# A gated attention and feed-forward stage: two interleaved streams become two half-programs, with taps and biases on TensorE

## The reference

```python
x1 = x + oT.T @ WoT0 + bo0                      # output of the cross attention before
n  = layernorm(x1)
q, k = elu(n @ Wq + bq) + 1, elu(n @ Wk + bk) + 1     # 16 heads of 16, per batch of 64 rows
v, g = n @ Wv + bv, sigmoid(n @ Wg + bg)
x1 = x1 + (g * (q @ masked_by_head(k.T @ v))) @ Wo + bo
xq = act_quant(layernorm(x1))                   # rounded to 127 / max|row|
h  = xq @ weight_quant(w1).T                    # 1024 wide
h  = silu(conv_w[:,0]*h[t-1] + conv_w[:,1]*h[t] + conv_w[:,2]*h[t+1] + conv_b)   # depthwise over 64 rows
x2 = x1 + act_quant(h) @ weight_quant(w2).T
q3 = layernorm(x2) @ Wq3 / 4                    # queries of the next stage
```

## Time and profile before

| | before |
|---|---|
| median of three runs | 3895.37 us (3893.12 to 3897.8) |
| profiled execution | 3894.62 us |
| its span, first to last instruction | 3892.6 us |
| granted TensorE clock over the span | 0.892 |
| busy: TensorE, VectorE, ScalarE, GpSimd | 3063.7, 2590.2, 1971.4, 620.4 us |

### The profile page before, as it was taken

One profiled execution on the slowest core, in us unless ns is written; L12 is line 12 of the kernel. 1 busy time (PEld: TensorE's weight loads), 2 busy tenths in 40 slices (PEclk: granted clock), 3 DMA queues, 4 the chain that ended last, 5 costly groups with the idle time before them and its releaser, 6 DMA issues. The chain is left out here.

```text
span 3892.6 us, 99208 instructions
## 1 busy us (share of the span) xinstructions
PE 3063.7 (79%) x34478; PEld 2671.8 (69%) x34478; DVE 2590.2 (67%) x7538; ACT 1971.4 (51%) x4188; POOL 620.4 (16%) x741
## 2 busy tenths in 40 slices
PE   3449999999999964555379999999999999643574
PEld 3348888888888853443268888888888888532453
DVE  5558888888888836666666777776777777465001
ACT  1146766666666632223246666666666666421111
POOL 0223333333333210000121111111111111000101
PEclk7669999999999986777679999999999999865787
DMA  2123223233333220000111111111111111212511
GB/s 66 50 82 84 82 79 85 80 82 83 81 82 83 67 62 11 22 22 11 36 32 42 38 42 39 38 40 40 39 38 41 38 42 28 73 44 69 191 48 61
DMA packets 235433, 221.17 MB, mean 57 GB/s; under 512 B 69516, under 2 KB 228545, under 8 KB 234816
## 3 DMA queue, kind: packets, MB, share of 16 engines
q1 hardware_dynamic: 232896, 208.22, 18.9%
q0 software_dynamic: 2048, 6.68, 0.5%
HBM read 186.30 MB, written 28.39 MB: 55 GB/s over the span
## 5 line engine op out<-in xcount | busy, mean ns | idle before, releaser
L1892 DVE CUSTOM_DVE_ANT_0 xb_junk<-xb_ring,xb_mbias 128x372 bf16<-128x372 f32 (+2 forms) x1024 | 543.6, 573 | 177.6 <-PE xb_ring L1800 158.0
L1731 ACT ACTIVATE xb_P<-xb_sc 124x1024 f32<-124x1024 f32 (+1 forms) x416 | 426.0, 1026 | 374.5 <-PE xb_sc L1824 372.6
L879 PE MATMUL xa_acc<-xa_raw,xa_P 124*128 124x193 f32 x1664 | 315.6, 331 | 7.7 <-ACT xa_P L754 7.7
L1771 PE MATMUL xb_ring<-xb_xst,xb_whi 128*128 128x372 f32 (+2 forms) x768 | 262.4, 369 | 38.6 <-DVE xb_xst L1871 32.8
L1800 PE MATMUL xb_ring<-xb_khi,xb_qhi 64*128 64x372 f32 (+2 forms) x1024 | 269.8, 404 | 26.4 <-DVE xb_klo L1877 17.3
L1771 PE MATMUL xb_ring<-xb_whi,xb_xst 128*124 128x256 f32 (+1 forms) x1248 | 285.3, 291 | 2.9 <-DVE xb_maxes L1892 0.6
L1824 PE MATMUL xb_sc<-xb_qhi,xb_khi 64*124 64x256 f32 (+1 forms) x1664 | 282.4, 372 | 0.0
L879 PEld LDWEIGHTS xa_acc<-xa_raw,xa_P 124*128 124x128 f32 x1664 | 266.4, 189 | 19.1 <-ACT xa_P L754 12.1
L1877 DVE TENSOR_TENSOR xb_klo<-xb_ring,xb_khi 128x372 fp32r<-128x372 f32 (+2 forms) x256 | 138.8, 572 | 208.7 <-ACT xb_khi L1697 207.7
L865 PE MATMUL xa_sc<-xa_qblk,xa_kT 128*124 128x128 f32 x1664 | 238.6, 272 | 0.0
L1771 PEld LDWEIGHTS xb_ring<-xb_whi,xb_xst 128*124 128x124 f32 (+1 forms) x1248 | 215.8, 187 | 23.0 <-DVE xb_maxes L1892 15.6
(11 more groups left out here) (418 smaller groups left out, 8222.9 us busy)
## 6 DMA issues: line engine op xcount, KB each, us to landing
xa_raw<-in_ctx SPq DMA_DIRECT2D x64, 279.0 KB
ex_w<-in_W SPq DMA_DIRECT2D x16, 1024.0 KB, 8.8
xa_raw<-in_ctx SPq DMA_DIRECT2D x32, 372.0 KB
xa_xTr<-in_ctxT SPq DMA_DIRECT2D x64, 186.0 KB
xb_raw<-in_ctxT SPq DMA_DIRECT2D x64, 186.0 KB
xa_xTr<-in_ctxT SPq DMA_DIRECT2D x32, 248.0 KB
xb_raw<-in_ctxT SPq DMA_DIRECT2D x32, 248.0 KB
xa_mask<-in_mask SPq DMA_DIRECT2D x32, 200.1 KB, 5.2
```

The costliest lines, as they stand in the source:

```text
L879: i = nc.tensor.matmul(acc[:, o, :], w, raw[0:KEYS, t3, t, :], start=t == 0 and o == 0, stop=t == NKT - 1, skip_group_check=True)
L1731: nc.scalar.activation(P[0:w, pbuf(c, p), :], sc[(c + p) % 2][0:w, :], ACT.Exp).then_inc(sem("exped"), 1)
L1771: i = nc.tensor.matmul(out, l, r, start=k == 0, stop=k == 4)
L1892: v.tensor_tensor_reduce(out=junk[:, k, 0:w], in0=ring[f % 3][:, 0:w], in1=mbias[:, p, k0:k0 + w], scale=1.0, scalar=-3.0e38, op0=ALU.add, ...
```

## The change

The streams and rounds go. All eight groups are written out, each as two half-programs, `attention(g)` and `ffn(g)`, and on every engine the halves of neighbouring groups are merged: each half is a generator that yields a planned time before every piece, attention of group g begins at 32g and its ffn at 32g + 31.5, and `by_time` always lets the half with the earliest next time go on. Attention has the banks pA to pD, the ffn pE to pH.

Work moves between engines. The biases of keys, values, gate and both output projections become a third matmul per tile (`row0`, one row of ones, against the bias). The three taps of the convolution become float32 matmuls with diagonal matrices `taps`, which GpSimd builds once. Elu reads PSUM on ScalarE (exp and relu), sigmoid and Silu become tanh: ScalarE writes y and tanh(y/2) from PSUM, VectorE multiplies y (1 + tanh); the factor 2 is taken out in the scales. GpSimd computes the power -0.5 of the variance in ln's and exp's place, and the rounding of the second quantization. The maximum over the ffn's values is taken in two halves. Loads come in two parts, `first` for attention and `later` for the ffn.

```diff
@@ helpers
+def by_time(*works):
+
+    nexts = [(begin + next(work), k) for k, (begin, work) in enumerate(works)]
+    while nexts:
+        _, k = at = min(nexts)
+        nexts.remove(at)
+        begin, work = works[k]
+        t = next(work, None)
+        if t is not None:
+            nexts.append((begin + t, k))
...
@@ gated_attention_and_ffn
+    EVERY, SECOND = 32, 31.5
...
+        def biased(out, xT, name, b):
+            for t in range(GROUP):
+                for k in range(2):
+                    nc.tensor.matmul(out[:, t, :], xT[:, k, TOK * t:TOK * t + TOK], wm[name][:, k, :], start=k == 0, stop=False)
+                i = nc.tensor.matmul(out[:, t, :], row0[:], bias[b][:], start=False, stop=True)
+            return i
+
+        def groups(*parts):
+
+            works = []
+            for g in range(NG):
+                works += [(g * EVERY + begin, part(g)) for begin, part in zip((0, SECOND), parts)]
+            by_time(*works)
...
@@ GpSimd
+                nc.gpsimd.tensor_tensor(b.rstd[:], b.var[:], mhalf[:], ALU.pow).then_inc(sem(tag + "_rstd"), 1)
...
+                    for f in range(NF):
+                        for k in range(3):
+                            i = nc.gpsimd.tensor_scalar(taps[:, f, k], ident[:], conv[:, f, k:k + 1], None, ALU.mult)
...
+                    nc.gpsimd.tensor_scalar(h2q[:, f:f + 2], h2r[:, f:f + 2], ROUND, ROUND, ALU.add, ALU.subtract).then_inc(sem("h2q"), 1)
...
@@ ScalarE
+                act.wait_ge(sem("k_ps"), g + 1)
+                nc.scalar.activation(ke[:], tok(pD), ACT.Exp)
+                nc.scalar.activation(kb[:], tok(pD), ACT.Relu).then_inc(sem("ke"), 1)
...
+                nc.scalar.activation(gb[:], tok(pB), ACT.Tanh, scale=0.5).then_inc(sem("gb"), 1)
...
-                    nc.scalar.activation(b.h2[:, f, :], b.cv[:, f % 3].rearrange("p b s -> p (b s)"), ACT.Silu).then_inc(b.sem("h2"), 1)
...
+                for f in range(NF):
+                    yield 5.2 + 1.7 * f
+                    act.wait_ge(sem("c_ps"), g * NF + f + 1)
...
+                    nc.scalar.activation(h2[:, f, :], c_bank(f), ACT.Identity, bias=conv[:, f, 3:4])
+                    nc.scalar.activation(th[:, f % 2], c_bank(f), ACT.Tanh, scale=0.5, bias=halfb[:, f:f + 1]).then_inc(sem("th"), 1)
...
@@ TensorE
+                for f in range(NF + 1):
+                    if f < NF:
+                        yield 3 + 1.7 * f
...
+                        for k in range(2):
+                            i = nc.tensor.matmul(h_bank(f), w1q[:, k, 128 * f:128 * f + 128], xqT[:, k, :], start=k == 0, stop=k == 1)
+                        i.then_inc(sem("h_ps"), 1)
+                    if f:
+                        yield 2.7 + 1.7 * f
+                        pe.wait_ge(sem("hs"), g * NF + f)
...
+                        for k in range(3):
+                            i = nc.tensor.matmul(c_bank(f - 1).rearrange("p (b s) -> p b s", s=S), taps[:, f - 1, k],
+                                                 padded[:, (f - 1) % 3, :, k:k + S], start=k == 0, stop=k == 2)
+                        i.then_inc(sem("c_ps"), 1)
...
@@ VectorE
-                v.tensor_tensor(b.kb[:], tok(b.pD), wide("bk"), ALU.add).then_inc(b.sem("kb"), 1)
...
-                v.tensor_tensor(b.vb[:], tok(b.pA), wide("bv"), ALU.add).then_inc(b.sem("vb"), 1)
...
-                    b.chain.step(v.scalar_tensor_tensor(out=b.cv[:, f % 3], in0=b.padded[:, f % 3, :, 0:S], scalar=conv[:, f, 0:1], in1=b.cv[:, f % 3], op0=ALU.mult, op1=ALU.add))
-                    v.scalar_tensor_tensor(out=b.cv[:, f % 3], in0=b.padded[:, f % 3, :, 2:S + 2], scalar=conv[:, f, 2:3], in1=b.cv[:, f % 3], op0=ALU.mult, op1=ALU.add).then_inc(b.sem("conv"), 1)
...
+                for f in range(NF):
+                    yield 3.7 + 1.7 * f
...
+                    v.tensor_tensor(padded[:, f % 3, :, 1:S + 1], h_bank(f).rearrange("p (b s) -> p b s", s=S),
+                                    srow[:].rearrange("p (b s) -> p b s", s=S), ALU.mult).then_inc(sem("hs"), 1)
+                    yield 6.2 + 1.7 * f
+                    dve.wait_ge(sem("th"), g * NF + f + 1)
+                    v.scalar_tensor_tensor(out=h2[:, f], in0=th[:, f % 2], scalar=1.0, in1=h2[:, f], op0=ALU.add, op1=ALU.mult).then_inc(sem("h2"), 1)
+                    if f == 5:
+                        yield 6.4 + 1.7 * f
+                        dve.wait_ge(sem("h2"), g * NF + NF // 2)
+                        v.tensor_reduce(top[:, 0], h2[:, 0:NF // 2].rearrange("p f t -> p t f"), AX.X, ALU.max, apply_absolute_value=True)
...
```

More of the change, by code:

```diff
@@ L1121, in _, with load @@
[L1121 to L1129 removed]
+            def load(g):
+                sp.dma_start(xs[:, g % 2], tiles_of(x, g)).then_inc(sem(f"x_in{g % 2}"), 16)
+                sp.dma_start(os_[:, g % 2], halves_of(oT, g)).then_inc(sem(f"x_in{g % 2}"), 16)
@@ L1131, in _ @@
+            load(0)
+            for dst, src in first:
+                sp.dma_start(dst, src).then_inc(sem("first_in"), 16)
+            for dst, src in later:
+                sp.dma_start(dst, src).then_inc(sem("later_in"), 16)
+            groups(attention, ffn)
+            for p in range(2):
+                sp.wait_ge(sem(f"x2_out{p}"), 16 * (NG // 2))
+                sp.wait_ge(sem(f"q3_out{p}"), 16 * (NG // 2))
         @block.gpsimd
         def _(pool):
+            nc.gpsimd.memset(row0[:], 0.0).then_inc(sem("zero"), 1)
@@ L1291, in work @@
[L1291 to L1297 removed]
+                i.then_inc(sem("y2_ps"), 1)
+                yield 34
+                pe.wait_ge(sem("c_norm"), g + 1)
+                transpose_group(nc, dim(pG), ln2, ident).then_inc(sem("l2_ps"), 1)
@@ L1298, in _ @@
+                yield 36
+                pe.wait_ge(sem("lT2"), g + 1)
+                by_dim(nc, dim(pG), lT2, wm["Wq3"]).then_inc(sem("q3_ps"), 1)
+            groups(attention, ffn)
         @block.vector
@@ new lines, in _, with variance @@
+            dve.wait_ge(sem("first_in"), FIRST)
+            dve.wait_ge(sem("set"), 1)
+            def variance(b, tag, X):
+                for t in range(GROUP):
+                    i = v.bn_stats(b.stats[:, t, :], X[:, t, :])
+                chain.step(i)
+                wait_apart(dve)
+                for t in range(GROUP):
+                    i = v.bn_aggr(b.moments[:, t, :], b.stats[:, t, :])
+                chain.step(i)
+                v.tensor_scalar(b.var[:], b.moments[:, :, 1], LN_EPS, None, ALU.add).then_inc(sem(tag + "_var"), 1)
@@ new lines, in ffn @@
+                for t in range(GROUP):
+                    i = v.scalar_tensor_tensor(out=X[:, t, :], in0=tok(pG)[:, t, :], scalar=s2[:, t:t + 1], in1=X[:, t, :], op0=ALU.mult, op1=ALU.add)
+                i.then_inc(sem("x2"), 1)
+                dve.wait_ge(sem("x2"), g + 1)
+                variance(nb2, "c", X)
+                yield 32
+                if g:
+                    dve.wait_ge(sem("l2_ps"), g)
+                normed(nb2, "c", X, ln2, g + 1)
+            groups(attention, ffn)
```

647 lines of the change are left out of this document (342 added, 305 removed).

## The result

The changed kernel takes **3959.3 us** in the median (3955.49 to 3961.17), against 3895.39 of the kernel before on the same chip: ratio 1.0162, 95% interval 1.0149 to 1.0174. It is slower, as forecast, but by 64 us where 24 were forecast, and outside the range.

A forecast was written before the change was run, and what follows sets the result against it. No engine was full; in the new order VectorE's program order would run eight tiles serially. The stage, 58 - 1.7 + 7 x 58.4 + 60.8 = 525.9 us against 502.0, gives +24: 3919 us, range 3880 to 3950.

The forecast's parts named there:

- Serial tiles: In the ffn's convolution, eight tiles run one after the other through three engines, 3.35 us each.
- From the first tap to Wo's residual add: Per group: 28.1 us for the eight tiles, 9.5 from there through Wo, and 1.2 for the clock.
- The 1.2 for Wo's clock: TensorE may lose its clock level ahead of Wo: +1.2 us per group, a mean of 0 and 2.6.
- From the diagonal to the first tap: Per group: diagonal 0.5 us, broadcast and y-projection 3.4, transposes to hidden pairs 3.9, y at half clock 2.5.
- GpSimd gets the rounding: Rounding 512 columns on GpSimd costs 0.61 us, four per group beside VectorE's row scalings; some 0.1 shows per group.
- the third rival: GpSimd decides: a power of 1.6 us exposed twice and the port, period 62, +49 us, 3944; chance 0.15.
- Wrong would make it: Signs against the forecast: tiles under 2.5 us apart, a power over 1.6 us, or a clock of 1.0 throughout.
- 24 of 0.3: At the stage's start, GpSimd builds 24 tap diagonals of 0.3 us ahead of the first power, ending at 27.5.
- The power: GpSimd's power -0.5 on 128x2: taken as 0.4 us, between 0.2 and 1.6, behind two roundings.
- The contention: VectorE's two-SBUF-input products wait for GpSimd's SBUF reads: 1.2 us per group by the rule, 0.3 by the measured row.
- The tail: The last group's ffn, with nothing beside it, up to the next stage: 60.8 us, 6.8 of it to its first taps.
- Costed at nothing: ... the bias matmuls, except ...: Bias matmuls cost nothing except between tiles 3 and 6 and in y and Wo, 0.86 us each.

The follow-up runs named there:

- e3: The changed kernel with VectorE's scaling of tile f+1 put ahead of the gating product of tile f: 3918.1 us, ratio 1.0056 to the kernel before.
- e4: The changed kernel with twelve added matmuls per group whose result nobody reads, between Wo and the next diagonal: 3939.6 us, ratio 1.0109 to the kernel before.
- e8: The changed kernel without the rounding of h2, the row scaling writing the BF16 tile directly (another result): 3923.4 us, ratio 1.0064 to the kernel before.
- e6: The changed kernel without the ten bias matmuls of a group (result lacks five projections' biases): 3929.9 us, ratio 1.0081 to the kernel before.

## Why the prediction was right in kind and wrong in size

The mechanism was right and one term of the sum far too small: what the work on GpSimd costs.

- **Serial tiles** (3.35 us): right, 3.28; e3 shows that the order causes it. The eight tiles with attention beside them were forecast at 28.1 and took 27.9.
- **From the first tap to Wo's residual add**, 28.1 + 9.5 + 1.2 = 38.8: measured 1853.23 - 1814.52 = 38.7. The 1.2 for Wo's clock was a mean of 0 and 2.6; Wo took 1.0 more than at full clock, 3.6 for 2.6, since its first half runs at half clock and its second at full. No line of the forecast names that case, so this agreement is luck in part.
- **From the diagonal to the first tap**, 0.5 + 3.4 + 3.9 + 2.5 = 10.3: measured 9.9. The clock's term was right: y at half clock, and e4 gives 2.1 of the 2.5 back.
- **"GpSimd gets the rounding": this step failed.** "A cast of 744 columns is 807 ns ... 512 columns are 0.61, and four lie beside VectorE's row scalings", with 0.1 exposed. Measured: 1.92 to 2.23 us, and 3.6 exposed per period (12.86 against 9.3), 8.1 in the tail. The rows of the cast are of one operation; this instruction has two (add, then subtract). The rounding was given one price and no upper end, though the text bounds the power from both sides: the upper end of 63 for a period has 3 us for all of GpSimd, and the third rival gives them to the power and the port. Nor is it among the signs of "Wrong would make it", none of which came. With e8's 33.0 us added, and the 0.7 that is there already taken off, the sum would have been about 3951.
- **"24 of 0.3": the same step at the start.** 0.58 each. The first power starts 1468.10 - 1432.97 = 35.1 us behind the first load, for 27.5: the late loads are in at 21.0 for 19.5, and the taps take 14.1 for 8.0 (24 of 0.3 are 7.2, so the 27.5 is 0.8 high by its own terms). So 6.1 of the head's 7.6 are the taps and 1.5 the loads; from the power to the diagonal it is 30.5, as forecast. The line through casts of 744 and 992 columns was carried down to 128. With these 7.6 on top of the 3951 it would have been 3959, and 3959.3 was measured; that it is so near is luck in part, since terms that were too high and too low cancel in the rest.
- **The power**: priced 0.4, measured 0.69 to 0.82, within its bounds; it is late mainly because it queues behind a rounding.
- **The contention** was worked out at 0.3 us per group and then left out of the sum, where 58.4 has 0.1 for all of GpSimd. The three row scalings grew from 1.89 (e8, which writes BF16; one alone takes 0.69 in both) to 2.30, the one-input pair L1438 from 0.73 to 1.43, and the small product L61 from 0.15 to 0.56. The Trainium skill (SBUF — State Buffer, Who interferes with whom) names both kinds, two SBUF inputs and the two-port modes of one-input operations; the trace agrees in kind, though no row tells the mode of L1438, and the forecast used only the first. In size it does not agree: by the rule as the prediction works it, two scalings would each wait for a rounding, here 1.9 us, and the three together grew by 0.4.
- **The tail** was forecast with 6.8 us from diagonal to first taps; it took 1936.28 - 1927.53 = 8.75, with the q3 projection at half clock (3.78 us). With the longer steps of the last two tiles this is more than the 1.3 that e8 leaves over. Some of e8's 8.1 is the clock's: without the roundings the first taps come after 7.69, and the last step of the tiles is 3.3 in place of 4.65.
- **The third rival** had the period, 62 for 61.4, by the power where it was the roundings, and a chance of 0.15. Its time, 3944, was too low because it kept the ends of the stage fixed ("117 + 7P"), while a dearer GpSimd lengthens both ends too: 7.6 and 9.5.
- **"Costed at nothing: ... the bias matmuls, except ..."**: right in sum. The four pairs that are counted (keys, values, y and Wo, 0.86 each) are 3.4; e6 has 3.0 per period on the path.

What stays open: how much of the rounding's 1.9 us is its second operation, and whether other unread matmuls would hold the clock in every group.

## What to carry to other kernels

Before work goes to another engine, look for a row of that very instruction there; if there is none, take the price of the nearest row times a factor as upper end (here the nearest rows were short by 3.1 and 1.9 times), and put it at every place where the engine is used, in the head and the tail too. When pieces of one generator keep their order, read which wait stands ahead of the instruction that feeds the next step: one swap (e3) was worth more than every other edit. And cut a measurement at fixed rows of the stage, since outside it these profiled runs differ by up to 12 us.
